# Hyperbolic attention: one of eight weight tiles as a power on GpSimd

## The reference, cut to what matters

```python
diff_sq = jnp.maximum(q_norm_sq + k_norm_sq - 2.0 * qk, 0.0)
denom = jnp.maximum((1.0 - CURV * q_norm_sq) * (1.0 - CURV * k_norm_sq), 1e-06)
cosh_arg = jnp.maximum(1.0 + 2.0 * CURV * diff_sq / denom, 1.0)
distance = jnp.where(cosh_arg > 1.0, jnp.arccosh(jnp.maximum(cosh_arg, 1.0 + 1e-12)), 0.0)
attn = jax.nn.softmax(-distance, axis=-1)
out = jnp.einsum('bhnm,bhmd->bhnd', attn, v)
```

## Time and profile before

| | us |
|---|---|
| median of 3 runs | 1426.32 |
| lowest and highest | 1423.31, 1429.2 |
| the profiled execution | 1425.32 |
| its span, first to last instruction | 1423.5 |
| the loop of the hyperbolic attention: first root to the end of the last weights | 789.9 to 1255.3 |

### The profile page before, as it was taken

The page is one execution under the profiler, slowest core; times in us unless marked ns, Lnnn a source line. Parts: engine busy times, 40 slices in busy tenths (PEclk is TensorE's granted clock), DMA queues, the critical chain, the costliest instruction groups (busy, mean ns, idle before and its releaser), DMA issues. The chain is left out here.

```text
span 1423.5 us, 17961 instructions
## 1 busy us (share of the span) xinstructions
PE 998.7 (70%) x5593; PEld 495.9 (35%) x5593; DVE 970.0 (68%) x2081; ACT 743.3 (52%) x848; POOL 467.6 (33%) x278
## 2 busy tenths in 40 slices
PE   5877624489999619995433677889888888444394
PEld 2453223156665519995210001111111111024393
DVE  6666696467776264453654999999999999336511
ACT  4204513225555504442230399999999999941031
POOL 0000000200000016652200577867876788200074
PEclk9987955679999758998565555555555555565587
DMA  4001000212110106673142010001000100020164
GB/s 139 0 6 21 1 0 19 78 46 78 35 37 18 38 28 214 219 205 92 40 132 81 22 40 27 23 23 37 28 23 23 42 24 0 0 62 5 44 181 120
DMA packets 67127, 80.11 MB, mean 56 GB/s; under 512 B 12692, under 2 KB 46110, under 8 KB 67042
## 3 DMA queue, kind: packets, MB, share of 16 engines
q1 hardware_dynamic: 58914, 68.83, 15.8%
q0 software_dynamic: 3968, 8.13, 1.9%
q10 hardware_dynamic: 4160, 2.10, 0.5%
HBM read 63.50 MB, written 15.34 MB: 55 GB/s over the span
## 5 line engine op out<-in xcount | busy, mean ns | idle before, releaser
L2373 POOL TENSOR_TENSOR hb_t<-hb_t,hb_r 128x1024 f32<-128x1024 f32 x124 | 326.7, 2671 | 205.7 <-ACT hb_r L2319 205.7
L2385 DVE TENSOR_SCALAR hb_dpos<-hb_psR 128x1024 f32<-128x1024 f32 x128 | 155.5, 1216 | 24.0 <-PE hb_psR L2248 19.3
L2257 PE MATMUL hb_psR<-ha_q,ha_k 20*128 20x512 bf16 x256 | 129.6, 606 | 55.8 <-DVE hb_dpos L2385 55.6
L2248 PE MATMUL hb_psR<-ha_q,ha_k 78*128 78x512 bf16 x256 | 130.1, 612 | 45.9 <-DMA ha_k<-hsx 40.8
L2393 DVE SCALAR_TENSOR_TENSOR hb_t<-hb_psR,hb_dpos 128x1024 f32<-128x1024 f32 x128 | 154.9, 1210 | 0.0
L2269 PE MATMUL hb_psO<-hb_t,ha_va 128*9 128x512 f32 x512 | 114.7, 996 | 45.5 <-ACT hb_t L2342 45.5
L1865 DVE TENSOR_REDUCE ga_nm<-ga_psA 128x1 f32<-128x128 f32 (+3 forms) x256 | 112.8, 484 | 47.1 <-PE ga_psA L1751 47.0
L1844 ACT ACTIVATE ga_att<-ga_psB 128x1024 f32<-128x1024 f32 (+3 forms) x128 | 86.9, 709 | 99.8 <-PE ga_psB L1776 99.8
L2402 DVE SCALAR_TENSOR_TENSOR hb_r<-hb_t 128x1024 f32<-128x1024 f32 x64 | 130.4, 2038 | 0.0
L2342 ACT ACTIVATE hb_t<-hb_t 128x4096 f32<-128x4096 f32 x32 | 113.8, 3602 | 0.0
L2319 ACT ACTIVATE hb_r<-hb_r 128x4096 f32<-128x4096 f32 x16 | 57.9, 3617 | 74.9 <-DVE hb_r L2402 74.8
(11 more groups left out here) (459 smaller groups left out, 2177.0 us busy)
## 6 DMA issues: line engine op xcount, KB each, us to landing
m2x_e_w<-in_L_ffn_W_dram SPq DMA_DIRECT2D x78, 256.0 KB
m1x_e_w<-in_L_ffn_W_dram SPq DMA_DIRECT2D x23, 256.0 KB
ga_q<-qx SPq DMA_DIRECT2D x48, 96.0 KB
ha_q<-hqx SPq DMA_DIRECT2D x48, 96.0 KB
ha_k<-hkx SPq DMA_DIRECT2D x16, 288.0 KB
hsx<-ha_aparts SPq DMA_DIRECT2D x6, 384.0 KB
hy_fwd<-in_const_fwd_dram SPq DMA_DIRECT2D x1, 2048.0 KB
f_down<-in_L_ffn_W_dram ACTq DMA_DIRECT2D x4, 512.0 KB, 3.9
```

The lines of the kernel that those rows point to most:

```text
L2248: mm = pe.matmul(psR[:, dist_slot(n), i, :], k[0:ROWS, it % 2, i0 + i, P * c:P * c + P], q[0:ROWS, it % 2, i0 + i, :], start=True, stop=True)
L2257: mm = pe.matmul(psR[:, side_slot(n), i, :], k[SIDE:SIDE + SROWS, it % 2, i0 + i, P * c:P * c + P], q[SIDE:SIDE + SROWS, it % 2, i0 + i, : ...
L2373: pool.tensor_tensor(tt, tt, r[:, (2 * it + form) % R_QUADS, k, :], ALU.add).then_inc(sum_ready, 1)
L2385: dve.tensor_scalar(dpos[:, n % 2, :], psR[:, dist_slot(n), :, :].rearrange("p i t -> p (i t)"), 0.0, None, ALU.max).then_inc(dpos_ready, 1)
```

## The change

- GpSimd, at the head of the loop's block, writes -2.0 into a tile of 128 x 1 and waits for it.
- In steps 0 to 14, behind the eight sums, GpSimd waits for the last of them (`sum_ready`) and raises the fourth unit of form 1 in place to the power of minus two: one tensor_tensor with the operation pow, 128 x 1024 f32, whose second operand is the constant broadcast over the columns. It raises `power_ready`.
- ScalarE's logarithm and exponential of form 1 take the first three units of the quad (128 x 3072) in these steps, and the logarithm waits for seven sums of the step instead of eight. Form 0 and the last step are as before.
- TensorE waits for `power_ready` too ahead of the values of chunk 3.

```diff
+            power_ready = s.sem("power_ready")
+            minus_two = s.sb("minus_two", [P, 1])
+            exponent_set = s.sem("exponent_set")
+            ROOTED = QUAD - 1
...
                     def values(it, c):
                         pe.wait_ge(w_ready, 2 * it + c % 2 + 1)
+                        if c == CH - 1 and it < STEPS - 1:
+                            pe.wait_ge(power_ready, it + 1)
...
+                    def unrooted(it, form):
+
+                        tt = quad(t, it, form)
+                        return tt[:, 0:ROOTED, :] if form == 1 and it < STEPS - 1 else tt
+
                     def logs(it, form):
-                        tt = quad(t, it, form)
+                        tt = unrooted(it, form)
                         if it == STEPS - 1 and form == 1:
                             act.wait_ge(late_sums, QUAD)
                         else:
-                            act.wait_ge(sum_ready, UNITS * it + QUAD * (form + 1))
+                            act.wait_ge(sum_ready, UNITS * it + QUAD * form + (QUAD if form == 0 else ROOTED))
...
                     def weights(it, form):
-                        tt = quad(t, it, form)
+                        tt = unrooted(it, form)
...
                 def _(pool):
+                    pool.memset(minus_two[:, :], -2.0).then_inc(exponent_set, 1)
+                    pool.wait_ge(exponent_set, 1)
                     for it in range(STEPS):
...
+                            if form == 1:
+                                pool.wait_ge(sum_ready, UNITS * it + UNITS)
+                                pool.tensor_tensor(tt, tt, minus_two[:, 0:1].to_broadcast([P, UN]), ALU.pow).then_inc(power_ready, 1)
```

## The result

The changed kernel takes **3743.64 us** (3 runs, 3743.3 to 3744.62) against 1426.32: 2.6247 times the time of before, with a 95% interval of 2.6179 to 2.6315. The forecast of 1417.5 was wrong, and so was its range, which ended at 1588. The profiled execution has a span of 3741.5 us.

The account below looks back on a forecast made before the run. ScalarE bounds eight of fourteen loop steps, VectorE the long six. Short steps save 7.0 us and the tail 1.7, 8.8 in all: 1425.3 to 1416.5, plus 1.0 for the median, 1417.5 us; range 1404 to 1588.

Parts of the forecast that it names:

- What bounds the loop: Hyperbolic loop: the larger of ScalarE's 27.58 us and VectorE's 26.56, or 28.79 where its second product collides with GpSimd.
- short steps: Eight of 14 loop steps, mostly 27.57 or 27.58 us, ScalarE without a gap; each forecast to gain 0.88 us.
- ScalarE's share: Logarithm and exponential of form 1 shortened: 1.73 us less a step; eight short steps and the tail gain 8.8 us.
- The term for TensorE: VectorE's clip waits for TensorE's distances behind form 0's exponential, so a short step is about 26.7 us, not 26.56.
- GpSimd's power: Fifteen 128x1024 powers behind the loop's sums: 2.3 to 5 us each, upper bound 18.1; only duration matters, not latency.
- The likeliest case: Power under 5 us, chance 0.50, 0.31 of it faster by over 0.5%; 1417.5 us, own range 1405 to 1434.
- it fits: Power under 5 us fits GpSimd's 5.0 us of idle time in a step of 26.7; chance 0.50.
- Rival A: GpSimd becomes the loop's bound, a step taking 21.7 us of sums plus the power: 1503 to 1588 us; chance 0.31.
- Its point of decision: Rival A's power duration, 6.5 us, from which GpSimd's sums and power decide against the mean step of 28.21 us.
- Rival B: Power of 5 to 8 us fits but collides with VectorE's four products: 8 us slower, 1434; chance 0.15.
- The estimate from a page: Power from 12 cycles an element at 1.2 GHz: 10.2 us, a step of 31.9, 52 us slower; not used in the sum.

Follow-up runs that it names:

- one multiplication: Changed kernel with GpSimd's power replaced by one multiplication by the broadcast constant, same tiles and waits: 1416.27 us, ratio 0.9937 to the kernel before.
- two multiplications: Changed kernel with GpSimd's power replaced by two multiplications by the constant, one behind the other: 1422.35 us, ratio 0.9986 to the kernel before.
- half a power: Changed kernel with the power over only the first 512 columns of the unit, the other 512 left as bare sum of roots: 2517.97 us.

## Why the prediction was wrong, step by step

- **What bounds the loop: right.** ScalarE in the short steps, VectorE at 26.56 and 28.79 us. Without the power the steps are 26.57 and 28.80.
- **ScalarE's share: right.** 1.73 us a step forecast; 0.85 in the logarithm (3.60 to 2.75) and 0.86 in the exponentials (7.11 to 6.25) measured. The forecast of 1417.5 for a power under 5 us met 1416.27 and 1416.53 with an operation of under 3 us, but that is luck in part. The prediction let an operation of under 3.1 us cost nothing and the short steps save 7.0 us. In the profiled execution with one multiplication, nine of the 14 steps are long, six before, and the 14 save 3.0 us; the first step saves 2.1, the tail 1.7, and the loop began 4.5 us sooner, at 785.3. That start lies anywhere from 785 to 794 us in the profiled executions of these kernels, though the work ahead of the loop is the same in all of them. The term for TensorE (0.14 us a step) was too large: without the power the clip idles 0.24 to 0.26 us in five steps, but a short step is 26.57, not 26.7.
- **GpSimd's power: the step that failed.** The prediction put its duration at 2.3 to 5 us and bounded it at 18.1; it is 163.2. It took the one iterated operation of another engine, VectorE's reciprocal, as 7.8 times its plain one, and carried the factor to GpSimd; there the power is 70 times the sum and 86 times a multiplication. It was another operation on another engine, and its row bounded nothing. Nor was the sum a lower bound: a multiplication over 128 x 1024 takes 1.89 us alone, the sum 2.32. And the value was taken from the instruction's form: the same TENSOR_TENSOR on the same shape. The form gives the traffic and not the work on an element.
- **The likeliest case.** With a price unknown between 2.3 and at least 18 us and 5 us to spare, the odds given were 0.50 for "it fits". The room was known to a tenth of a microsecond, the price not to a factor of seventy; an honest range had to be open at the top. Rival A was the right mechanism and its line held where its price was put in: steps of 30.3 us forecast for 8.6 us, 30.2 measured, though the collisions alone would make as much there. For 163.2 it gives a step of 184.9, 183.8 measured; it leaves out the fifteenth power ahead of the last sums, 140 us. Its point of decision, 6.5 us, lies between the 4.8 us that show no loss and the 8.7 that do.
- **Rival B.** Its collisions show at a small price: with two multiplications (4.8 us) a further product collides, and the gain is lost to that. It is right that a product can wait for a power, and wrong on how long. Of some 163 us it is held at most 82.0, not all of p, and a power of 512 columns holds a product 0.7 us. These waits, most of the 1183.3 us of VectorE's products, cost next to nothing here (10 us at most by half a power), since GpSimd's own rate was the bound.
- **The estimate from a page.** The Trainium skill's "GPSIMD Engine Reference" (Performance versus the Vector engine), with its 12 cycles an element, gave an estimate of 10.2 us; measured are 163.2, sixteen times that, and the measurement decides. No run shows whether the power is a body of the kind that the figure is for.

## What to carry to other kernels

When work is moved to an engine with so much room to spare, the whole question is the price of the one new operation there; if no row shows it, the shape of the instruction is no guide to it, and a probe of one instruction settles it before any schedule is changed. Give a price that is unknown an open end, and don't put the forecast on the side that needs it to be small. An engine's busy time in the page can double by waiting alone (VectorE's here): read the group with its least and greatest duration (1.21 and 78.22 us for VectorE's products) before calling it work.

## What the runs showed of the hardware

- GpSimd's pow in f32 takes 0.159 us a column: 163.2 us for 1024. At 256 columns it is 41.1 us for five exponents (-2, 2, 1, 0.5, -1), for inputs of 1.0, for a broadcast and a full second operand and for 128, 64, 16 and 4 partitions. A multiplication over 128 x 1024 takes 1.89 us alone.
- VectorE's instruction with two SBUF inputs waits for a running GpSimd power only until about 512 columns of it are left: 0.7 us for 512, 82.0 for 1024, 244.6 for 2048. Instructions behind it run at full rate beside the rest of the power (1.21 us at 1084.65). One with a single SBUF input isn't held: L2409 at 1003.12, with its other input in PSUM, takes its 1.21 us while the power of 999.05 runs.
- The power pays nothing for the product that it holds: the one of 999.05 lasts 163.23 us, and 163.26 alone. Only where a product was already running when a power started is the power longer: 164.07 us (started at 1385.30) for 163.26, 82.49 (started at 1271.49) for 81.91.
